# A decoder layer on one core: the query projection of the cross attention made four units earlier, and what follows from it moved along

## What is computed

```
q = Wq @ x + bq;  k = Wk @ ctx + bk;  v = Wv @ ctx + bv      # 256 x 512 per batch element
dot = q_h . k_h / 4                                          # 16 heads of 16 rows, 512 x 512 each
dot = mask * dot - (1 - mask) * 1e6
amap = softmax(dot, axis=-1) * mask
out = amap @ v_h;  x = layernorm(x + out)
```

## Time and profile before

| | us |
|---|---|
| median of 3 runs | 3369.53 |
| the runs | 3376.11, 3364.22, 3369.53 |
| profiled execution: its time | 3367.53 |
| profiled execution: span from first to last instruction | 3365.7 |
| the attention phase in it: starts of the first and the last product for the maxima | 1854.8 and 2886.6 |

### The profile page before, as it was taken

One profiled execution on the slowest core, in us unless ns is written; L12 is line 12 of the kernel. 1 busy time (PEld: TensorE's weight loads), 2 busy tenths in 40 slices (PEclk: granted clock), 3 DMA queues, 4 the chain that ended last, 5 costly groups with the idle time before them and its releaser, 6 DMA issues. The chain is left out here.

```text
span 3365.7 us, 46151 instructions
## 1 busy us (share of the span) xinstructions
PE 3051.1 (91%) x16134; PEld 1828.5 (54%) x16134; DVE 2789.0 (83%) x2773; ACT 2407.5 (72%) x4531; POOL 2093.1 (62%) x1207
## 2 busy tenths in 40 slices
PE   7899999999999999999985799899999999879998
PEld 5677667766776667666754334344343433234444
DVE  6999999999999998999997777677777777378886
ACT  4877788778787877778774267566666666657776
POOL 5999989999999999999987134333433433200000
PEclk9999999999999999999997799999999999989999
DMA  4012210222022202221123545554555464131111
GB/s 166 31 43 76 76 56 30 76 76 79 8 79 76 76 13 73 76 76 32 55 91 99 162 140 154 166 171 146 169 172 168 138 182 143 46 116 45 45 45 35
DMA packets 164376, 311.86 MB, mean 93 GB/s; under 512 B 22736, under 2 KB 80208, under 8 KB 164000
## 3 DMA queue, kind: packets, MB, share of 16 engines
q1 hardware_dynamic: 158784, 299.53, 27.9%
q10 hardware_dynamic: 5360, 9.38, 1.1%
HBM read 217.16 MB, written 91.69 MB: 92 GB/s over the span
## 5 line engine op out<-in xcount | busy, mean ns | idle before, releaser
L820 POOL TENSOR_TENSOR bu<-du,bc 128x1024 f32<-128x1024 f32 x512 | 1196.7, 2362 | 82.6 <-DMA bc<-bc_scratch 70.8
L698 ACT ACTIVATE states<-dt,negA 128x256 f32<-128x256 f32 x2048 | 852.2, 463 | 359.7 <-DVE hc L917 334.5
L904 DVE TENSOR_TENSOR_SCAN states<-states,bu 128x1024 f32<-128x1024 f32 x352 | 805.9, 2289 | 73.8 <-ACT states L698 69.1
L1556 DVE TENSOR_REDUCE mmax<-s_ps 128x2 f32<-128x1024 f32 x512 | 624.5, 1224 | 256.0 <-PE s_ps L1275 239.7
L1400 ACT ACTIVATE pt<-s_ps 128x512 f32<-128x512 f32 x1024 | 572.9, 596 | 339.7 <-PE s_ps L1284 330.7
L917 DVE TENSOR_TENSOR hc<-states,bc 128x1024 f32<-128x1024 f32 x352 | 430.8, 1224 | 41.1 <-DVE states L904 6.4
L518 PE MATMUL y_ps<-id_sb,hc 128*128 128x128 f32 x2816 | 380.2, 279 | 83.7 <-DVE hc L917 83.7
L518 PEld LDWEIGHTS y_ps<-id_sb,hc 128*128 128x128 f32 x2816 | 323.9, 143 | 209.6 <-DVE hc L917 171.0
L1284 PE MATMUL s_ps<-qst,kst 105*128 105x512 bf16 x1024 | 381.2, 388 | 11.7 <-ACT pt L1400 5.1
L829 POOL TENSOR_TENSOR hp<-hp,bc 128x1024 f32<-128x1024 f32 x160 | 377.6, 2360 | 16.3 <-DVE hp L904 16.0
L1275 PE MATMUL s_ps<-kst,qst 102*128 102x512 bf16 x1024 | 320.9, 396 | 57.2 <-DMA kst<-mask_d 46.7
(11 more groups left out here) (172 smaller groups left out, 4247.0 us busy)
## 6 DMA issues: line engine op xcount, KB each, us to landing
bc<-bc_scratch SPq DMA_DIRECT2D x128, 512.0 KB, 7.8
stack_d<-parts SPq DMA_DIRECT2D x180, 256.0 KB, 3.0
qst<-stack_d SPq DMA_DIRECT2D x64, 384.0 KB
kst<-stack_d SPq DMA_DIRECT2D x64, 384.0 KB
x<-xres SPq DMA_DIRECT2D x31, 512.0 KB, 4.9
w_raw<-in_w_ffn SPq DMA_DIRECT2D x48, 256.0 KB, 2.7
w_raw<-in_w_ffn SPq DMA_DIRECT2D x16, 768.0 KB, 7.3
xT_sb<-in_xT SPq DMA_DIRECT2D x16, 512.0 KB, 3.3
```

The lines of the kernel that those rows point to most:

```text
L698: a = act.activation(states[:, bank, first:first + SEQ], dt[:, t, :], ACT.Exp, scale=negA[:, t, c * NS + n:c * NS + n + 1])
L820: pool.tensor_tensor(bu[:, buf, :].rearrange("p (n l) -> p n l", n=NS), du[:, t % (2 * GRP):t % (2 * GRP) + 1, :].to_broadcast([P, NS, SEQ ...
L904: m = dve.tensor_tensor_scan(dst, src, bu[:, BU_OF[k][0], half * 2 * SEQ:(half + n) * 2 * SEQ], 0.0, ALU.mult, ALU.add)
L1556: dve.tensor_reduce(mmax[:, u // HG, c:c + 2], s1_ps[:, pair], AX.X, ALU.max).then_inc(s1_free, 1)
```

## The change

The two query projections stand in units 3 and 4 (before: 3 and 8). The four "turn" steps stand in units 5 to 8 (before: 4 to 7). The first step "m" stands in unit 9 and the first step "back" in unit 10 (before: 10 and 9). The query parts are made in units 8 and 9 (before: 10 and 11). o_sb has five buffers in place of four, used in rotation, so that the first copy of a pass does not wait for the "turn" steps; the second one does. SP issues the row maxima of groups 0 and 1 behind the loads of groups 0 and 1. Two steps of `quantise` go from units 8 and 9 to 10 and 11.

```diff
+OSB = HGROUPS + 1
-MISC = ((0, "m", 2, 0), (1, "k", 0, 2), (2, "k", 1, 2), (3, "q", 0, 2), (4, "turn", 0, -1),
-        (5, "turn", 1, -1), (6, "turn", 2, -1), (7, "turn", 3, -1), (8, "q", 1, 2), (9, "back", 0, -1),
-        (10, "m", 0, 1), (11, "v", 0, 1), (12, "v", 1, 1), (13, "back", 1, -1), (14, "m", 1, 1))
+MISC = ((0, "m", 2, 0), (1, "k", 0, 2), (2, "k", 1, 2), (3, "q", 0, 2), (4, "q", 1, 2),
+        (5, "turn", 0, -1), (6, "turn", 1, -1), (7, "turn", 2, -1), (8, "turn", 3, -1), (9, "m", 0, 1),
+        (10, "back", 0, -1), (11, "v", 0, 1), (12, "v", 1, 1), (13, "back", 1, -1), (14, "m", 1, 1))
-SPLIT_AT = {"k": 4, "q": 10}
+SPLIT_AT = {"k": 4, "q": 8}
-        o_sb = sb("o_sb", [P, HGROUPS, HID])
+        o_sb = sb("o_sb", [P, OSB, HID])
@@ SP @@
-                if active(s):
-                    max_rows(s, 1 - par, 0)
                 if active(f):
                     wait(q_split, f)
                     store_parts(0)
...
                 group(0)
                 group(1)
+                if active(s):
+                    max_rows(s, 1 - par, 0)
                 group(2)
@@ ACT, copy_values @@
-                if g == 0 and not (isinstance(b, int) and b == 0):
+                if g == 1 and b > 0:
                     act.wait_ge(mm["turn"], b * TT)
-                act.activation(o_sb[:, g, :], pv_ps[:, :], ACT.Copy).then_inc(o_copied, 1)
+                act.activation(o_sb[:, (b * HGROUPS + g) % OSB, :], pv_ps[:, :], ACT.Copy).then_inc(o_copied, 1)
@@ POOL, quantise @@
-                elif u == 8:
+                elif u == 10:
...
-                elif u == 9:
+                elif u == 11:
```

More of the change, by code:

```diff
@@ L1341, in shared @@
                     for g in range(HGROUPS):
-                        product(misc[:, g * P:(g + 1) * P], o_sb[:, g, idx * P:(idx + 1) * P], id2[:, :])
+                        product(misc[:, g * P:(g + 1) * P], o_sb[:, (batch * HGROUPS + g) % OSB, idx * P:(idx + 1) * P], id2[:, :])
                 elif kind == "back":
```

## The result

| | before | after |
|---|---|---|
| median of the runs | 3371.07 (4 runs) | 3313.78 (4 runs) |
| lowest and highest | 3364.22 to 3376.11 | 3310.60 to 3314.32 |
| span of the profiled execution | 3365.7 | 3308.8 |

The ratio is 0.9829, with a 95% interval of 0.9810 to 0.9848: 57 us, or 1.7%, faster. The forecast was 3314. Run again in a later job, the changed kernel had 3310.9, at a ratio of 0.9829 (0.9812 to 0.9845).

A forecast was written before the change was run, and what follows sets the result against it. Passes were held up by waits for operands and context, from a late query chain. Terms 20.8 + 12.0 + 14.2 + 5.1 + 3.5 = 55.6 us gave 3311.9 profiled, 3314 as median; range 3300 to 3338.

The forecast's parts named there:

- What bounds the kernel: Attention phase, passes 1 to 13: PE waits for stacked operands and context because the query chain runs too late.
- Query chain: Queries ready near 39.2 us into a pass, loads issued at 45.5; PE's operand waits go wholly, 20.8 us.
- Context: Issued near unit 14, lands by 67, likely 65 to 66; PE's wait goes, 12.0 us, bounds 0 and 12.
- Rival A: Context stays late, its delay not coming from the crowd of loads; 3328 us, chance 0.14.
- Clock: Without waits of 2 us and more, PE's clock stays up in passes 1 to 13; 14.2 us.
- First pass: Pass 0 begins behind a wait for the same operands; its chain moves forward likewise, 5.1 us.
- Order of the shared steps: Units 4 to 11 come to 30.1 us instead of 30.39, 3.5 us gained in 13 passes.
- The waits and the clock: Passes 1 to 13: operand waits 20.8, context waits 12.0 and lowered clock 14.2 us all go.
- rival D: Waits go but PE's pass doesn't shrink, as DVE or ACT caught up in them; half the gain, 3341, chance 0.07.
- B: ACT's rounding in unit 8 waits for the keys' stores, 0.6 us in hand; 3334 us, chance 0.08.
- C: SP's maxima store behind 1.6 MB of loads lands too late; near 3393 us, chance 0.05.
- E: Change doesn't do what it says, chain gated by something unseen; time stays at 3369 us, chance 0.04.

The follow-up runs named there:

- e1: Changed kernel with SP storing the row maxima of groups 0 and 1 ahead of the queries again; 3314.9 us, ratio 0.9848.
- e7: Kernel before with second query projection in unit 4, turns in 5 to 8, fifth buffer; query parts still in units 10 and 11; 3358.8 us, ratio 0.9966.
- e4: Changed kernel with ACT's copy to o_sb put ahead of the rounding in units 4 and 8; 3297.2 us, ratio 0.9794; 3296.5 in a later job.
- e3: Kernel before with only the fifth buffer of o_sb added; 3364.4 us, ratio 0.9989.
- e2: Kernel before with only SP's row maxima moved behind the loads of groups 0 and 1; 3440.5 us, ratio 1.0215.
- e5: e4's kernel with query parts made in units 9 and 10 instead of 8 and 9, maxima still behind the loads; 3361.6 us, ratio 0.9983.
- e9: e4's kernel with SP storing the maxima ahead of the queries; 3302.7 us, ratio 0.9799.

## Why the prediction was right

The time came out as forecast (3314), and by the mechanism forecast; that it hit so closely took some luck, as the last points show. Point by point:

**What bounds the kernel.** Late operands and a late context, from one cause. Shown: both waits are gone in after and, but for 2.1 us, in e1; e7, which has the moved projection and the fifth buffer without the earlier chain, keeps both.

**Query chain.** Ready at 39.2 was the forecast, loads at 45.5; in after the queries are ready at 40.1 in most passes and the loads go out at 46.3 to 47.6. The wait of 20.8 us fell to nothing. e1, with loads at 52 to 55, has none either, so there are 6 us and more in hand.

**Context.** Forecast: landing at 65 to 66 in the pass, 12.0 us gone. It landed at 64.7 to 67.0 in the twelve of these passes that load one, and nothing waited. Rival A, that its delay doesn't come from the crowd, is out: its landing went 11.0, 9.4, 7.2 us as SP's loads ahead of it grew fewer (before, e1, after). The Trainium skill (DMA: Bandwidth & Descriptors, Queues, rings and completion order) has the engines take turns between queues; by that rule, as I read it, the landing would not have hung on what SP's queue holds, and the three landing times speak against that reading. The packets show where the rule holds and where it doesn't. These are the DMA queues in pass 8 of before, first in the 4 us behind the issue of the context (2499.39 to 2503.39), then in the 4 us behind those (2503.39 to 2507.39; SP's queue is q1, ACT's q10; packets, MB, share of the 16 engines):

```profile
q1 hardware_dynamic: 337, 1.02, 98.6%
...
q1 hardware_dynamic: 207, 0.59, 60.9%
q10 hardware_dynamic: 222, 0.44, 43.7%
```

At first nothing of the context moves, and SP's queue has the engines to itself; then the two queues share them packet by packet, 222 to 207, much as that section of the Trainium skill has it. The time from the issue to the context's first packet is 4.2 us in the median before, 5.0 in e1 and 3.2 in after; from there to the landing it is 7.1, 4.2 and 4.0. So e1 and after differ in the first part, and before differs from e1 in the second, where more loads are beside it. What holds back the first packet, no run shows.

**Clock.** 14.2 us were forecast; PE's busy time in the thirteen passes fell by 804.4 - 787.5 = 17.0, at a clock of 1.00 throughout. Of this, 14.2 is the fall to the 60.79 us that pass 8 of before has at a clock of 1.00; the other 2.8 is that a pass of after is busy for 60.57 us at the same clock, and is no matter of the clock. The forecast was right, though not its bound of 2 us: in before the granted clock fell to 1.2 GHz also behind two waits for the context of 1.9 us (passes 5 and 11), and in e7 behind one of 1.7.

**First pass.** 5.1 us were forecast from the wait; the stretch from the first product for the maxima to the start of pass 1 shrank by 8.2 us (1854.8 to 1977.0 before, 1851.8 to 1965.8 after).

**Order of the shared steps: a term that was mis-sized.** I had -3.5 us and a pass of 61.9; the pass is 62.4. Units 4 to 11 of pass 8 now take 2450.20 - 2419.84 = 30.36 us, where they took 30.39 and I had 30.1. Over the thirteen passes they take 395.2 us, as before (395.3): the term came to nothing. (Its bounds were added wrongly, too: -10 and +9 stood in place of the -3.5, so the range from them was 3307 to 3327 and not 3304 to 3323.) The windows of units 0, 8 and 11 of pass 8 after, against the earlier trace rows, and behind them unit 0 of pass 8 before:

```profile
2402.64:2406.12 3.48, 3.27 (x17) 0.94 (x17) 2.35 (x3) 2.46 (x6) 0.00 (x0) 1.00 0.22 82
...
2434.80:2439.29 4.49, 3.36 (x22) 1.42 (x21) 3.07 (x5) 3.46 (x7) 2.13 (x1) 1.00 0.00 0
...
2445.92:2450.20 4.28, 4.28 (x24) 2.10 (x23) 3.26 (x4) 3.06 (x6) 3.97 (x4) 1.00 0.80 253
...
2439.38:2442.42 3.04, 3.04 (x19) 0.86 (x17) 2.09 (x2) 1.74 (x4) 0.00 (x0) 1.00 1.05 254
```

Unit 11 is 4.28, as worked out (4.3). Unit 8 is 4.49 and not 4.27: the wait for the copy grew to 1.13, where I had 0.95. For the rest, unit 4 is 0.08 longer than I had, units 9 and 10 together 0.08, and unit 5 is 0.09 shorter. That the fifth buffer would not take the wait away but ACT's rounding would fill its place was right; e4 shows it by taking the rounding out of the way.

**The waits and the clock: the other term that was mis-sized.** Together they were to give 20.8 + 12.0 + 14.2 = 47.0 us. Units 12 to 15 and 0 to 3, where they lie, shrank by 459.4 - 416.1 = 43.3 us in the thirteen passes. A cause is in unit 0, 3.48 us where pass 8 of before had 3.04. The window of pass 8 before stands last above. PE's timeline at the start of pass 8 after:

```profile
2403.61 1.07 PE L1296 MATMUL pv_ps<-pt,vaug 128*32 128x512 f32 x8 [0.19 <-ACT o_sb L1442]
```

PE waits 0.19 us for a copy to o_sb there, where in before it had none: ACT had caught up while PE stood waiting for operands. The other 0.25 us of the difference lies in the same place, ahead of the value products: they begin 0.97 us into the pass, in before 0.53 (the second exponential product waits for ACT too). So the unit had been short because it followed a stall, and I took its length for the normal one. The traces bear this out. In before, e3 and e7 unit 0 takes 3.04 us (once 3.12) in every pass that begins behind a wait with the clock at 1.00 in it; in the thirteen passes of after and of e1, none of which begins behind a wait, it takes 3.49 each time. That is 0.45 us a pass, or 5.8 in thirteen, which the stalls had been giving back; smaller things went the other way, as two waits of 0.9 us for ACT at the end of a pass, which I had not counted. It is a small piece of rival D.

**The sum.** The thirteen passes gave 43.3 us (854.6 to 811.3) and not 50.5: 3.5 are missing from the order and 3.7 from the waits and the clock. What made up for it was the first stretch, 3 us more than I had, and 5.4 us nearly all in code that the change doesn't touch: the first product for the maxima began 3.0 us sooner, and what follows the last one was 2.4 shorter (479.1 to 476.7). Without the 5.4 the forecast would have been some 4 us too low; that it hit to the microsecond is luck, that it hit to 10 is not.

**Rivals.** B (the rounding waits for the keys' stores): the last store of the keys lands 1.7 us ahead of the rounding in ten of the thirteen passes, and 0.1 ahead in two; in one of these, pass 6, ACT does wait for it, and the wait in unit 8 is 1.28 instead of 1.13. No more than that. C (maxima too late) did not come in the changed kernel and is real, as e2 and e5 show; its landing took 5.4 to 7.3 us of the 11.5 that I had given it. D fell but for the piece in unit 0; E fell.

## What to carry to other kernels

In an in-order pipeline with the same work in each pass, look for the stretch in which the DMA engines are idle and for the crowd behind it: here a chain of rounding, storing and loading began late for one projection's sake, and moving that projection four units paid mostly through what it let start sooner. Where one in-order queue serves several chains, price each chain's slack together: the same exchange of two entries on SP cost 71 us alone and gained a little behind an earlier chain. And when a wait is removed, look at what else stands ahead of the waited-for instruction on its engine; exchanging two neighbours on ACT gave as much as a quarter of the whole change.

## What the runs showed that I had not expected

A small store pays for the large loads issued ahead of it: 24 KB of maxima mostly took 1.5 to 1.7 us to land with no load ahead (before, e1), 5.4 to 7.3 behind two groups of loads (after) and 8.2 in pass 8 of e2. The 12 KB of group 2 took up to 10.7 before, behind three groups and the result, with the context beside them. In the thirteen passes the clock fell only behind waits for a DMA, at the start of a pass or for the context in its unit 1 (in before, seven times, behind waits of 1.9 to 5.1 us): in after, where no wait was over 1.3 us, PE's busy time was 60.5 to 60.7 us in each, against 60.8 to 63.2 before. Unit 0 alone, 3.04 us behind a stall at full clock, took 4.6 to 5.6 in before where the clock had fallen. And the parts of the program that no kernel here touches differ by up to 4.7 us ahead of the phase and 3.4 behind its last product for the maxima between the profiled executions, which is more than several of the edits were worth. It needn't all be chance: the phase begins at 1853.8 to 1854.8 in before, e2, e3, e5 and e7, and at 1850.1 to 1851.8 in the seven others but e9 (1854.5). The cause stays open.
